# Cross attention with its second scores computed with keys on partitions, in a two-layer decoder

## What is computed

```
q, k, v = heads(LN(x) @ Wq + bq), heads(ctx @ Wk + bk), heads(ctx @ Wv + bv)
energy  = where(mask, q @ k.T / scale, -1e9 or -1e20)      # 112 x 375 per head
x       = x + (softmax(energy) @ v) @ Wo + bo
```

## Time and profile before

| | |
|---|---|
| median of 3 runs | 2185.32 us (2185.08 to 2186.77) |
| the profiled execution | 2182.53 us |
| its span, first to last instruction | 2181.2 us |
| mean granted TensorE clock | 0.971 |
| TensorE, matmuls | 2019.4 us busy, 93% |
| VectorE | 1128.5 us, 52% |
| ScalarE | 801.1 us, 37% |
| GpSimd | 287.6 us, 13% |
| cross attention, layer 0 and layer 1 | about 641 to 1005 us, and 1245 to 1612 us |

### The profile page before, as it was taken

One profiled execution on the slowest core, in us unless ns is written; L12 is line 12 of the kernel. 1 busy time (PEld: TensorE's weight loads), 2 busy tenths in 40 slices (PEclk: granted clock), 3 DMA queues, 4 the chain that ended last, 5 costly groups with the idle time before them and its releaser, 6 DMA issues.

```text
span 2181.2 us, 34256 instructions
## 1 busy us (share of the span) xinstructions
PE 2019.4 (93%) x12672; PEld 1300.4 (60%) x12672; DVE 1128.5 (52%) x3152; ACT 801.1 (37%) x1802; POOL 287.6 (13%) x263
## 2 busy tenths in 40 slices
...
DMA packets 125987, 53.57 MB, mean 25 GB/s; under 512 B 108552, under 2 KB 117760, under 8 KB 125056
## 3 DMA queue, kind: packets, MB, share of 16 engines
...
## 4 chain that ended last, share of the span: by engine, by line
PE 75%; DVE 13%; issue 6%; ACT 4%; POOL 1%; DMA 1%; SPq 0%; DVEq 0%; ACTq 0%; POOLq 0%
PE ps L1775 18%; PE ps L491 6%; PE ps L1099 6%; PE ps L1477 5%; PE ps L1762 5%; PE ps L1085 5%; PE ps L1151 4%; PE ps L1128 4%; PE ps L554 3%; PE ps L1783 3%; PE ps L615 2%; DVE big_b L754 2%; DVE h_w L1299 2%; PE ps L1145 2%; PE ps L1197 2%
## 5 line engine op out<-in xcount | busy, mean ns | idle before, releaser
L1235 ACT ACTIVATE h_w<-h_w 112x375 f32<-112x375 f32 x512 | 304.3, 602 | 73.7 <-DVE h_w L1299 69.9
L1299 DVE CUSTOM_DVE_ANT_0 h_w<-ps,h_w 112x375 f32<-112x375 f32 x512 | 263.5, 544 | 58.8 <-PE ps L1085 53.0
L1099 PEld LDWEIGHTS ps<-ident,h_w 112*125 112x125 f32 x1536 | 187.3, 188 | 92.8 <-issue 79.7
L1099 PE MATMUL ps<-ident,h_w 112*125 112x112 f32 x1536 | 233.5, 288 | 1.1 <-ACT h_w L1243 0.6
L1243 ACT ACTIVATE h_w<-ps 125x336 f32<-125x336 f32 x384 | 169.8, 443 | 151.5 <-PE ps L1099 151.0
L754 DVE SCALAR_TENSOR_TENSOR big_b<-ps,taps,big_b 128x444 f32<-128x444 f32 (+2 forms) x288 | 194.1, 674 | 24.9 <-ACT big_b L679 10.6
L1775 PE MATMUL ps<-big_a,h_w 128*128 128x448 f32 x512 | 193.5, 540 | 3.4 <-DVE big_a L1822 3.4
L1775 PE MATMUL ps<-big_b,h_w 128*128 128x448 f32 x512 | 193.5, 540 | 0.7 <-ACT big_b L1801 0.7
L1830 DVE TENSOR_TENSOR xn<-ps,w_s 112x512 f32<-112x512 f32 x8 | 5.2, 686 | 299.4 <-PE ps L1783 299.4
L1775 PEld LDWEIGHTS ps<-big_a,h_w 128*128 128x128 f32 x512 | 97.0, 190 | 99.9 <-issue 93.7
L1775 PEld LDWEIGHTS ps<-big_b,h_w 128*128 128x128 f32 x512 | 96.9, 190 | 95.6 <-issue 93.7
...
## 6 DMA issues: line engine op xcount, KB each, us to landing
...
blocks<-h_w SPq DMA_DIRECT2D x128, 12.2 KB
...
```

What stands on the lines that cost most here:

```text
L1099: ins = pe.transpose(ps[0:CK, 4 + r % 2, c * T:(c + 1) * T], k.P[H % RING][:, c * CK:(c + 1) * CK], k.ident[0:T, 0:T])
L1235: act.activation(P, P, ACT.Exp, scale=-1.0, bias=k.neg_max[:, H % RING:H % RING + 1]).then_inc(s["exp"], 1)
L1299: dve.tensor_tensor_reduce(k.P[H % RING], ps[0:T, r, 0:S2], k.mask_add[n % 2], -1.0, 3.0e38, ALU.add, ALU.min, k.neg_max[:, H % RING:H % R ...
```

## The change

The weights are no longer turned on TensorE. The scores are computed a second time, with keys on partitions, and the exponential is taken of these; the first scores serve for the maxima alone.

- `scores` and `maximum` stay, but what `maximum` writes beside the maxima (`k.masked`) is read by nobody, and the negated maxima go to a column of `k.neg_max` that belongs to a spare row of the head's row group. `maxima` transposes that tile (one transpose a quad), and `less_maximum` on VectorE adds the result to the quad's queries (`k.Qx`), which so have the negated maximum in the spare row.
- The keys are stored twice, `k.Kx[z]`, each with the rows of the other head zero and the spare row one (`k_keep`, `k_bias`). So the second product, `turned` (twelve matmuls a quad with 32 rows, 125 keys and 112 queries each, four row groups side by side), gives scores less their maximum. First and second scores share banks 0 to 5 (`score_bank`, `turned_bank`).
- ScalarE takes the exponential of it out of PSUM into `PTx`, four a quad; there are no copies of weights.
- The mask is applied to the exponentials. `mask_rows` on VectorE makes a mask of ones and zeros (`mask01`, ones where a row's `mask_add` has its largest value), TensorE turns it in three pieces (`mask_turn`), ScalarE copies it as float and as int32. VectorE takes the minimum of one head's exponentials and the mask, GpSimd multiplies the other three heads' bits with it as int32. `apply` waits for these.
- TensorE's step is now: scores of Q, `maxima` of Q-1, early piece, `turned` of Q-1, `apply` of Q-2, late piece. ScalarE does the pieces' copies first and the four exponentials last. On VectorE `less_maximum` leads and `weights` ends a step.

```diff
+def score_bank(Q, r):
+    return (8 * Q + r) % POOL_BANKS
+def turned_bank(Q, r):
+    return (8 * Q + 12 + r) % POOL_BANKS
...
     def scores(seq, q):
         n, m, z = base + seq, q // 2, q % 2
+        Q = 4 * n + q
         if q == 0:
-            pe.wait_ge(s["k_sb"], 2 * (n + 1))
+            pe.wait_ge(s["k_sb"], 4 * (n + 1))
             pe.wait_ge(s["qz"], n + 1)
         for r in range(4):
-            H = 4 * (4 * n + q) + r
-            if H >= 4:
-                pe.wait_ge(s["max"], H - 3)
+            if r < 2 and Q:
+                pe.wait_ge(s["max"], 4 * Q - 1 + r)
+            elif r >= 2 and Q >= 2:
+                pe.wait_ge(s["exp"], 4 * Q - 9 + r)
             rows = slice(32 * r, 32 * r + 32)
-            pe.matmul(ps[0:T, r, 0:S2], k.Qz[n % 2][rows, z, m, :], k.Kx[n % 2][rows, m, :],
+            pe.matmul(ps[0:T, score_bank(Q, r), 0:S2], k.Qz[n % 2][rows, z, m, :], k.Kx[n % 2][rows, z, m, :],
                       start=True, stop=True).then_inc(s["S"], 1)
-    def turn(seq, q, r):
+    def maxima(seq, q):
         Q = 4 * (base + seq) + q
-        H = 4 * Q + r
-        pe.wait_ge(s["exp"], H + 1)
-        if r < 2 and Q:
-            pe.wait_ge(s["PT_act"], 3 * (Q - 1) + 2 + r)
-        elif r == 2:
-            pe.wait_ge(s["PT_act"], 3 * Q + 1)
-        elif r == 3:
-            pe.wait_ge(s["PT_dve"], Q + 1)
+        pe.wait_ge(s["max"], 4 * Q + 4)
+        if Q:
+            pe.wait_ge(s["exp"], 4 * Q - 1)
+        pe.transpose(ps[:, turned_bank(Q, 0), NC * T:(NC + 1) * T], k.neg_max[:, q % 2, :], k.ident[0:T, 0:T]).then_inc(s["max_T"], 1)
+    def turned(seq, q):
+        n, m, z = base + seq, q // 2, q % 2
+        Q = 4 * n + q
+        pe.wait_ge(s["qx"], Q + 1)
+        if Q:
+            pe.wait_ge(s["exp"], 4 * Q)
+        if Q < last:
+            pe.wait_ge(s["max"], 4 * Q + 6)
         for c in range(NC):
-            ins = pe.transpose(ps[0:CK, 4 + r % 2, c * T:(c + 1) * T], k.P[H % RING][:, c * CK:(c + 1) * CK], k.ident[0:T, 0:T])
-        ins.then_inc(s["PT_ps"], 1)
+            for r in range(4):
+                rows = slice(32 * r, 32 * r + 32)
+                ins = pe.matmul(ps[0:CK, turned_bank(Q, r), c * T:(c + 1) * T], k.Kx[n % 2][rows, z, m, c * CK:(c + 1) * CK],
+                                k.Qx[Q % 2][rows, :], start=True, stop=True)
+                if c == NC - 1:
+                    ins.then_inc(s["ST"], 1)
     def apply(seq, q):
         n = base + seq
         Q = 4 * n + q
-        pe.wait_ge(s["PT_act"], 3 * (Q + 1))
-        pe.wait_ge(s["PT_dve"], Q + 1)
+        pe.wait_ge(s["weights0"], Q + 1)
+        pe.wait_ge(s["weights"], 3 * (Q + 1))
...
+    def mask_turn(n, chunks):
+        pe.wait_ge(s["mask01"], n + 1)
+        for i, c in enumerate(chunks):
+            ins = pe.transpose(ps[0:CK, 7, (KD + i) * T:(KD + i + 1) * T], k.mask01[:, c * CK:(c + 1) * CK], k.ident[0:T, 0:T])
+        ins.then_inc(s["mask_T_ps"], 1)
     def norm_turn(seq):
         n = base + seq
-        pe.wait_ge(s["k_sb"], 2 * n + 2)
+        pe.wait_ge(s["k_sb"], 4 * n + 4)
         pe.wait_ge(s["c_xn"], n + 1)
+        mask_turn(n, (0,))
...
         if is_sequence(seq):
             scores(seq, q)
-        for r in range(2):
-            if is_sequence(before):
-                turn(before, b_q, r)
+        if is_sequence(before):
+            maxima(before, b_q)
         piece(seq, q, False)
+        if is_sequence(before):
+            turned(before, b_q)
         if is_sequence(ago):
             apply(ago, a_q)
-        for r in range(2, 4):
-            if is_sequence(before):
-                turn(before, b_q, r)
         piece(seq, q, True)
...
     def weights(seq, q, r):
-        H = 4 * (4 * (base + seq) + q) + r
-        P = k.P[H % RING]
-        act.wait_ge(s["max"], H + 1)
-        act.activation(P, P, ACT.Exp, scale=-1.0, bias=k.neg_max[:, H % RING:H % RING + 1]).then_inc(s["exp"], 1)
-    def copy(seq, q, r):
         Q = 4 * (base + seq) + q
-        act.wait_ge(s["PT_ps"], 4 * Q + r + 1)
+        act.wait_ge(s["ST"], 4 * Q + r + 1)
         if Q >= 2:
             act.wait_ge(s["PV"], Q - 1)
-        act.activation(k.PTx[(4 * Q + r) % RING], ps[0:CK, 4 + r % 2, 0:NC * T], ACT.Copy).then_inc(s["PT_act"], 1)
+        act.activation(k.PTx[(4 * Q + r) % RING], ps[0:CK, turned_bank(Q, r), 0:NC * T], ACT.Exp).then_inc(s["exp"], 1)
     def keys(seq, m):
         n = base + seq
         act.wait_ge(s["k_proj"], 2 * n + m + 1)
         if n >= 2:
-            act.wait_ge(s["S"], XH * (n - 1))
-        if l == 0:
-            ins = act.activation(k.Kx[n % 2][:, m, :], ps[:, 7, 0:S2], ACT.Copy)
-        else:
-            ins = act.activation(k.Kx[n % 2][:, m, :], ps[:, 7, 0:S2], ACT.Identity, bias=k.xb_col[:, 1, m:m + 1])
-        ins.then_inc(s["k_sb"], 1)
+            act.wait_ge(s["ST"], XH * (n - 1))
+        if l and n == base and m == 0:
+            act.wait_ge(s["k_bias"], 1)
+        for z in range(2):
+            bias = k.k_bias[:, 2 * m + z:2 * m + z + 1] if l else k.k_keep[:, 2 + z:3 + z]
+            act.activation(k.Kx[n % 2][:, z, m, :], ps[:, 7, 0:S2], ACT.Identity, scale=k.k_keep[:, z:z + 1],
+                           bias=bias).then_inc(s["k_sb"], 1)
...
     def maximum(seq, q, r):
         n = base + seq
-        H = 4 * (4 * n + q) + r
+        Q = 4 * n + q
         if q == 0 and r == 0:
             dve.wait_ge(s["mask"], n + 1)
-        dve.wait_ge(s["S"], H + 1)
-        if H >= RING:
-            dve.wait_ge(s["PT_ps"], H - RING + 1)
-        dve.tensor_tensor_reduce(k.P[H % RING], ps[0:T, r, 0:S2], k.mask_add[n % 2], -1.0, 3.0e38, ALU.add, ALU.min,
-                                 k.neg_max[:, H % RING:H % RING + 1]).then_inc(s["max"], 1)
-    def copy(seq, q):
-        Q = 4 * (base + seq) + q
-        dve.wait_ge(s["PT_ps"], 4 * Q + 2)
+        if r == 0 and Q >= 2:
+            dve.wait_ge(s["max_T"], Q - 1)
+        if 4 * Q + r >= 2:
+            dve.wait_ge(s["max"], 4 * Q + r - 1)
+        dve.wait_ge(s["S"], 4 * Q + r + 1)
+        at = 32 * r + (XD if q % 2 == 0 else 0)
+        dve.tensor_tensor_reduce(k.masked[r % 2], ps[0:T, score_bank(Q, r), 0:S2], k.mask_add[n % 2], -1.0, 3.0e38, ALU.add, ALU.min,
+                                 k.neg_max[:, q % 2, at:at + 1]).then_inc(s["max"], 1)
+    def less_maximum(seq, q):
+        n, m, z = base + seq, q // 2, q % 2
+        Q = 4 * n + q
+        dve.wait_ge(s["max_T"], Q + 1)
         if Q >= 2:
-            dve.wait_ge(s["PV"], Q - 1)
-        dve.tensor_copy(k.PTx[(4 * Q + 1) % RING], ps[0:CK, 5, 0:NC * T]).then_inc(s["PT_dve"], 1)
+            dve.wait_ge(s["ST"], 4 * (Q - 1))
+        dve.tensor_tensor(k.Qx[Q % 2], k.Qz[n % 2][:, z, m, :], ps[:, turned_bank(Q, 0), NC * T:(NC + 1) * T], ALU.add).then_inc(s["qx"], 1)
+    def weights(seq, q):
+        n = base + seq
+        Q = 4 * n + q
+        if q == 0:
+            dve.wait_ge(s["mask_T"], 2 * n + 2)
+        dve.wait_ge(s["exp"], 4 * Q + 1)
+        P = k.PTx[4 * Q % RING]
+        dve.tensor_tensor(P, P, k.mask_T[n % 2], ALU.min).then_inc(s["weights0"], 1)
+    def mask_rows(seq):
+        n = base + seq
+        dve.wait_ge(s["mask"], n + 1)
+        dve.tensor_reduce(k.mask_max, k.mask_add[n % 2], AXX, ALU.max).then_inc(s["mask_max"], 1)
+        dve.wait_ge(s["mask_max"], n + 1)
+        if n:
+            dve.wait_ge(s["mask_T_ps"], 2 * n)
+        dve.tensor_scalar(k.mask01, k.mask_add[n % 2], k.mask_max, None, ALU.is_ge).then_inc(s["mask01"], 1)
...
+        if is_sequence(before):
+            less_maximum(before, b_q)
         if is_sequence(seq):
             maximum(seq, q, 0)
-        if is_sequence(before):
-            copy(before, b_q)
-        if is_sequence(seq):
             maximum(seq, q, 1)
             maximum(seq, q, 2)
...
+            mask_rows(seq + 1)
+        if is_sequence(before):
+            weights(before, b_q)
...
+    def weights(seq, q, r):
+        n = base + seq
+        Q = 4 * n + q
+        if q == 0 and r == 1:
+            pool.wait_ge(s["mask_T"], 2 * n + 2)
+        pool.wait_ge(s["exp"], 4 * Q + r + 1)
+        P = k.PTx[(4 * Q + r) % RING]
+        pool.tensor_tensor(P.bitcast(I32), P.bitcast(I32), k.mask_I[n % 2], ALU.mult).then_inc(s["weights"], 1)
+    for step in range(-QUADS, (B + 1) * QUADS):
+        seq, q = quad_at(step)
+        before, b_q = quad_at(step - 1)
+        if q == 0 and is_sequence(seq + 1):
+            n = base + seq + 1
...
+        if is_sequence(before):
+            for r in range(1, 4):
+                weights(before, b_q, r)
...
+    a["k_keep"] = np.stack([other == 0, other == 1, np.arange(128) % 32 == XD, np.arange(128) % 32 == 0], 1).astype(f)
```

More of the change, by code:

```diff
@@ L181, in room @@
         return t[:, 0:n] if dt == F32 else t.bitcast(dt)[:, 0:n]
-    k.P = [room(S2, 0, parts=T) for _ in range(8)]
+    k.masked = [room(S2, 0, parts=T) for _ in range(2)]
     k.PTx = [room(NC * T, 0, parts=CK) for _ in range(8)]
@@ L1046 @@
 RING = 8
+POOL_BANKS = 6
```

106 lines of the change are left out of this document (65 added, 41 removed).

## The result

| | before | after |
|---|---|---|
| median | 2185.2 us (2182.5 to 2186.8, 4 runs) | 2259.9 us (2258.1 to 2261.2, 4 runs) |
| ratio, 95% interval | | 1.034 (1.033 to 1.036) |
| span of the profiled execution | 2181.2 us | 2259.9 us |
| mean granted TensorE clock | 0.971 | 0.961 |

A forecast was written before the change was run, and what follows sets the result against it. TensorE sets the pace and would wait on VectorE's chain: 2 layers x (14 x (22.84 - 21.94) + 7) = 39 us on 2182.5, plus 2.8 for the median, said as 2225. Range 2186 to 2290; own range 2200 to 2245.

The forecast's parts named there:

- (c): Rival: GpSimd becomes the bound, int32 multiplies at 1.50 us giving 2286 us; chance 0.13, and 0.05 for yet slower multiplies.
- The chain of 2.50 us: In each step, TensorE's turned scores wait for VectorE's less_maximum and first two maxima until 2.50 us after the scores' start.
- q0: TensorE's step from a sequence's first score group to its second, predicted at 5.43 us.
- q1: TensorE's step from a sequence's second score group to its third, predicted at 5.14 us, 5.45 with the port lock.
- the handover: Last term of the wait before the turned scores, behind VectorE's second maximum: 0.05 us.
- keys(1) at 3.7 (wanted at 4.06): hidden: ScalarE's key copies for the second half of keys would be ready before TensorE wants them, adding no wait.
- The 0.31 for the lock: GpSimd's multiply holds VectorE's minimum through the shared port at q0's end, making less_maximum late and q1 0.31 us longer.
- The ends: Start and finish of each cross attention layer: about +7 us a layer, 4 to 10.
- (a): Rival: TensorE stays the bound, faster; waits vanish and 1.7 us a sequence are saved, 2152 us; chance 0.10.
- (b): Rival: about the same; turned scores cost 0.71 us, the lock nothing, only the ends count, 2189 to 2199; chance 0.15.
- (d): Rival: the turned scores' weight loads don't overlap over row groups, 2.9 us in place of 0.85, about 2450; chance 0.02.
- (e): Rival: TensorE's clock falls because of the pauses, 2250 us or more; chance 0.03.

The follow-up runs named there:

- Half maxima: The changed kernel with VectorE's maxima taken over only the last 187 of 375 keys: 2215.8 us, ratio 1.013.
- `less_maximum` third: The changed kernel with VectorE's less_maximum put behind the first two maxima instead of ahead of them, same work: 2233.5 us, ratio 1.022.
- third-buffer kernel with the mask on ScalarE: The changed kernel plus a third key buffer, the 0/1 mask made by ScalarE instead of VectorE's comparison, and VectorE's minimum ahead of the norm: 2234.7 us, ratio 1.023.
- third-buffer kernel: The changed kernel with a third buffer for the doubled keys, so key copies no longer wait for the previous sequence's last turned scores: 2338.0 us, ratio 1.069.
- short multiplies: The changed kernel with a third key buffer and GpSimd's multiplies over 168 of their 336 columns: 2242.8 us, ratio 1.027.
- half the columns: The changed kernel, still with two key buffers, with GpSimd's multiplies over 168 of 336 columns: 2255.2 us, ratio 1.032.
- the kernel with both orders: The changed kernel with third key buffer, 0/1 mask on ScalarE, less_maximum behind two maxima, and apply ahead of the turned scores in two steps: 2193.7 us, ratio 1.004.

## Why the prediction was right, and where it wasn't

**Right in sign and mechanism, in range by luck.** 2225 was forecast in 2186 to 2290, 2259.9 came: 75 us more than before where 40 had been forecast. That is outside the 2200 to 2245 of my own mechanism. It is inside the wide range only since that was drawn to take in (c), a bound by GpSimd, which didn't come. The forecast was that TensorE's work falls and its waits grow by more, and that is what the rows show: matmuls 2019 to 1990 us busy, 85% in the stage as said. It was the likeliest case, with a term missing: the wait of the key copies for their buffer, put at nothing.

**The chain of 2.50 us.** Measured 2.57 in q0 (943.91 to 946.48) and 2.54 in q1 (950.31 to 952.85). Its terms held: `less_maximum` at 1.18 (0.83 + 0.43 = 1.26 predicted) taking 0.27 (0.26); the turned block 0.86 (0.85), 946.48 to 947.34. The second maximum ended at 2.41 (945.78 and 0.54), so the handover was 0.16 in place of 0.05. q3 came within 0.04, q2 within 0.04 in layer 0; in layer 1 q2 has 0.13 more, for the four instructions that VectorE's queries take there. Half maxima and `less_maximum` third show the mechanism.

**The step that failed: "They feed q1's early piece at 1.35 and keys(1) at 3.7 (wanted at 4.06): hidden."** The copies' duration was right (0.660 in the groups, 0.65 predicted), but I asked only when their data would come and not when their place comes free. What the second half of `keys` waits for was forecast for 3.7 us into q0, and its start for 4.06; it started at 4.94. The change moves the last reader of a key buffer from the first scores of q3 to the turned scores of q3, which stand in the next step. The copies start at 947.58, 3.67 into q0, the second half of `keys` can't start before 948.85, and q0 becomes 6.40 in place of 5.43. In the third-buffer kernel with the mask on ScalarE q0 is 5.59 and `keys` doesn't wait. The 0.97 that q0 has over the forecast is 27 us in 28 sequences, more than the 23 that the sum lacked inside the layers (48.3 us measured against 25). The 0.31 for the lock, which never came, made up for 8 of it, and the small excess in q2 and q3 took back 4.

**The lock was put in the wrong place.** I had it lengthen q0's minimum to 1.4 and q1 by 0.31. The minimum was never held: 0.49 at 949.59, 505 ns in the mean. It was GpSimd that waited there. Its first multiply was issued at 949.56, while the comparison ran (to 949.67), and VectorE's minimum followed at 949.59 without a gap; that multiply took 1.28, the three 2.99 in place of 2.61. 28 multiplies were held so, 1.28 to 1.38 us; the longest of all 384 took 1383 ns, the median one 897:

```profile
L1498 POOL TENSOR_TENSOR h_w<-h_w x384: 888/897/1383, 672.9 to 1681.8; 125x336 int32<-125x336 int32 x192
```

q1 was 5.17, near the 5.14 without a lock. The lock is real all the same: once the key wait was gone, it held the comparison, an operation with one input that I had costed at 0.54 and left out of the argument, for 2.55 us more. In these two kernels the side that was in kept the other out as long as its next operation followed at once: VectorE in the kernel after, GpSimd in the one with three key buffers. With the short multiplies it was not so to the end. I had looked at single operations where series count. And that the comparison went free in the kernel after hung on a pause of 0.10 us, which I hadn't looked at.
The Trainium skill, "SBUF — State Buffer", Who interferes with whom, has the port pair as an exclusive lock; the 3.08 us agree with that, and the 2.99 us too.

**GpSimd.** A multiply took 0.897 us in the median and 0.926 in the mean, with the held ones (0.93 predicted), and GpSimd was busy 58% (60%). int32 costs it what its float32 rows gave for this size. At half the columns the steps didn't move, so rival (c) is out.

**The exponentials** took 457 ns (0.44).

**The ends: 14 predicted, 30 measured.** The parts were named (three multiplies in a row, the mask's chain, second key copies), and the multiplies at the end are there:

```profile
1039.35 1.48 ACT L1278 ACTIVATE h_w<-ps 125x336 f32<-125x336 f32 x4 [2.98 <-PE ps L1129]
...
1040.22 2.59 POOL L1498 TENSOR_TENSOR h_w<-h_w 125x336 int32<-125x336 int32 x3 [1.86 <-ACT h_w L1278]
...
1042.96 0.78 PE L1145 MATMUL ps<-h_w 125*32 125x112 f32 x24 [2.91 <-POOL h_w L1498]
```

TensorE waits 2.91 us for them. The groups' starts divide the 30. From the last score group to the last residual addition it is 19.6 us in layer 0 and 17.7 in layer 1, before 14.6 in both: 8.0, where 4 had been forecast. The first sequence of a layer is 3.2 and 4.0 longer (2.3 forecast). The last one, up to its last score group, is 3.1 and 2.2 longer, and for it I had put nothing. Ahead of the first scores it is 3.0 in layer 0, and 5.6 between the two cross attentions (2.7 forecast for each layer). Some 1.2 are left. In many of these stretches the clock is lower, too: over the execution 180 us were at 0.5, before 130. Around layer 0 it is at 0.5 from 627.5 to 665.1 and again from 1023.5 to 1037.1 and from 1044.0 to 1074.7; before, from 629.9 to 660.7 and from 1008.8 to 1036.1. How much of the 30 is the clock, and how much waits, no run shows.

**Rivals.** (a), TensorE stays the bound: 1.7 us a sequence were to be had if the chain didn't wait, and the kernel with both orders has 0.5 to 0.7 of them; the time was then eaten by the ends. (b) asked for a cheaper turned block, which was 0.86, and for a lock that costs nothing, which came true. (d) is out by the same row. (e): the clock in the stage stayed at 1.00 with TensorE 85% busy in pauses of up to 1 us. It fell to 0.5 in the third-buffer kernel, at 909.7, behind a pause of 1.72 us (907.45 to 909.16) and with another of 1.01 at hand, and that was more than half of what q1 grew there.
